# Feed-forward stage: the last group's maxima by one strided reduction, the last products by groups over four banks, the next stage's first rows and weights in the last turn

## The reference

```python
def act_quant(x):
    scale = 127.0 / jnp.clip(jnp.max(jnp.abs(x), axis=-1, keepdims=True), 1e-05)
    return jnp.clip(jnp.round(x * scale), -128, 127) / scale
...
def bit_linear(x, w):
    xq = x + jax.lax.stop_gradient(act_quant(x) - x)
    wq = w + jax.lax.stop_gradient(weight_quant(w) - w)
    return jnp.einsum('bsd,hd->bsh', xq, wq)
...
h = bit_linear(x, w1)
h = depthwise_conv1d(h.transpose(0, 2, 1), conv_w, conv_b)
h = h.transpose(0, 2, 1)
h = jax.nn.silu(h)
return bit_linear(h, w2)
...
x = x + jnp.tanh(g_ffn[0]) * _L0_ffn_ref(_layernorm(x, axis=-1), L0_ffn_w1, L0_ffn_conv_w, L0_ffn_conv_b, L0_ffn_w2)
```

## Time and profile before

| | us |
|---|---|
| three runs | 2578.31, 2588.45, 2589.29 |
| their median | 2588.45 |
| the profiled execution | 2587.03 |
| its span, first to last instruction | 2585.2 |
| feed-forward stage in it, about | 989 to 1520 |
| one turn in the loop, about | 62.5 or 63.9 |

### The profile page before, as it was taken

The page is one execution under the profiler, slowest core; times in us unless marked ns, Lnnn a source line. Parts: engine busy times, 40 slices in busy tenths (PEclk is TensorE's granted clock), DMA queues, the critical chain, the costliest instruction groups (busy, mean ns, idle before and its releaser), DMA issues. The chain is left out here.

```text
span 2585.2 us, 40732 instructions
## 1 busy us (share of the span) xinstructions
PE 2362.0 (91%) x16307; PEld 1554.4 (60%) x16348; DVE 1443.2 (56%) x1747; ACT 1060.5 (41%) x1228; POOL 608.7 (24%) x208
## 2 busy tenths in 40 slices
PE   8899999999999987899999878898878999999989
PEld 6655554555555543444444346676656888888867
DVE  7665646556565545777777567878544222222235
ACT  5444445444454442555554534444423221121223
POOL 0045546455464651000000013323210000000000
PEclk9899999999999988999999989999879999999999
DMA  9410101101010103111111131212322000000046
GB/s 298 178 40 12 49 10 48 43 11 47 10 48 11 56 15 123 34 50 49 49 53 38 38 112 44 83 56 87 106 85 82 33 32 26 22 32 32 17 156 218
DMA packets 102015, 163.73 MB, mean 63 GB/s; under 512 B 16997, under 2 KB 39525, under 8 KB 99103
## 3 DMA queue, kind: packets, MB, share of 16 engines
q1 hardware_dynamic: 95918, 150.82, 17.6%
q10 hardware_dynamic: 6000, 11.54, 1.2%
HBM read 112.63 MB, written 49.71 MB: 63 GB/s over the span
## 5 line engine op out<-in xcount | busy, mean ns | idle before, releaser
L1135 DVE TENSOR_REDUCE att_mx<-att_sn 128x2 f32<-128x1024 f32 x256 | 313.6, 1225 | 168.4 <-PE att_sn L947 166.0
L1047 ACT ACTIVATE att_num<-att_st 128x2048 f32<-128x2048 f32 x128 | 240.5, 1879 | 149.8 <-PE att_st L935 93.3
L860 POOL TENSOR_TENSOR att_es<-att_es,att_num 128x2048 f32<-128x2048 f32 x64 | 294.8, 4606 | 15.0 <-ACT att_num L1047 8.8
L856 POOL TENSOR_TENSOR att_es<-att_num 128x2048 f32<-128x2048 f32 x32 | 145.8, 4557 | 375.8 <-PE att_pj L917 366.4
L2508 ACT ACTIVATE rec_ga<-rec_g,rec_bg 128x512 f32<-128x512 f32 x84 | 57.1, 687 | 307.8 <-PE rec_g L2409 307.8
L2409 PE MATMUL rec_g<-weights_a_h,row_weights_h 128*128 128x512 f32 x384 | 152.9, 398 | 13.6 <-ACT rec_ga L2508 11.1
L2409 PE MATMUL rec_g<-weights_a_l,row_weights_h 128*128 128x512 f32 x384 | 151.7, 395 | 0.0
L2409 PE MATMUL rec_g<-weights_a_h,row_weights_l 128*128 128x512 f32 x384 | 151.5, 395 | 0.0
L947 PE MATMUL att_sn<-att_kh,att_qh 32*128 32x512 f32 x512 | 127.3, 493 | 22.7 <-DVE att_mx L1135 22.7
L1708 DVE TENSOR_TENSOR ffn_hs<-ffn_h,ffn_fb 128x1024 f32<-128x1024 f32 x64 | 78.1, 1220 | 117.5 <-PE ffn_h L1454 108.9
L561 POOL TENSOR_TENSOR ffn_ln_rstd<-ffn_ln_var,ffn_ln_power 128x4 f32<-128x4 f32 x8 | 22.0, 2755 | 484.0 <-DVE ffn_ln_var L582 484.0
(11 more groups left out here) (399 smaller groups left out, 5699.3 us busy)
## 6 DMA issues: line engine op xcount, KB each, us to landing
rows<-in_x SPq DMA_DIRECT2D x16, 1024.0 KB, 5.5
rows<-x SPq DMA_DIRECT2D x16, 1024.0 KB, 5.2
rows_b<-in_fside_BxSxS SPq DMA_DIRECT2D x8, 1024.0 KB, 7.9
heads<-att_o SPq DMA_DIRECT2D x32, 256.0 KB, 2.3
weights_b_l<-heads SPq DMA_DIRECT2D x8, 1024.0 KB, 5.2
x<-ffn_xr SPq DMA_DIRECT2D x32, 256.0 KB, 2.1
xat_xr<-x SPq DMA_DIRECT2D x8, 1024.0 KB, 5.1
out_x<-x SPq DMA_DIRECT2D x8, 1024.0 KB, 8.8
```

What stands on the lines that cost most here:

```text
L856: pool.tensor_tensor(ES[:], E[0][:], E[1][:], ALU.add).then_inc(s_sum, 1)
L860: pool.tensor_tensor(ES[:], ES[:], E[k][:], ALU.add).then_inc(s_sum, 1)
L1047: act.activation(E[k][:], st_ps[:], ACT.Exp, scale=SCALE).then_inc(s_exp, 1)
L1135: dve.tensor_reduce(MX[c % 2][:, m // 2, 2 * DH * (m % 2):2 * DH * (m % 2) + DH + 1:DH], sn_ps[:], AX, ALU.max, negate=True).then_inc(s_ma ...
```

## The change

- `absolute(b, 3)`, the ACT pass over the last group, is gone, and so is `magnitude(b, 3)` on DVE. In their place DVE folds AM first (groups 0 to 2) and then runs `last_maxima`: one `tensor_reduce` with absolute values over the last group, read as 512 rows of 4 values that lie 2048 bytes apart, into AB[:, 0], and one `tensor_tensor` of 512 elements into AM[:, 0].
- Batch 7's second product runs by groups: for each group, four matmuls into each of four banks (a, b and the two of h), behind one wait for each group.
- The next stage's `ln.moments` and `ln.scale` move from the tail into turn 7 on DVE; ACT's two high parts move ahead of `second_row(7)`; the two low parts on DVE move ahead of and behind the four `rounded`; SP issues the two weight loads ahead of the stores of batch 6.
- ACT's copy of XM into XR for batch 7 moves from ahead of the four `whole` to between the second and the third.

```diff
-        MAX_N = GROUPS + 1
+        MAX_N = GROUPS + 2
...
-            turn(B - 1, True, False, False)
             sp.wait_ge(s_h, B * PAIRS)
             for i, next_w in enumerate((next_wq, next_wo)):
                 sp.dma_start(raw[i], kxn(next_w)).then_inc(s_nextw[i], 16)
+            turn(B - 1, True, False, False)
...
+            def last_products():
+                banks = (a_ps[:], b_ps[:], h_ps[:, 0, :], h_ps[:, 1, :])
+                pe.wait_ge(s_qb, B)
+                for group in range(GROUPS):
+                    pe.wait_ge(s_quant, (B - 1) * GROUPS + group + 1)
+                    for t in range(T):
+                        for i in range(HG * group, HG * group + HG):
+                            last = pe.matmul(banks[t], SQ[:, i, t * P:t * P + P], W2[:, i, :],
+                                             start=(i == 0), stop=(i == HT - 1))
+                        if group == GROUPS - 1:
+                            last.then_inc(s_y, 1)
...
-                absolute(b, 3)
...
             turn(B - 1, True, False, False)
-            second_row(B - 1)
-            act.wait_ge(s_store, (B - 1) * T * 16)
-            act.wait_ge(s_xm, B)
-            act.activation(XR[:], XM[:], ACT.Copy).then_inc(s_xr, 1)
-            for group in range(GROUPS):
-                whole(B - 1, group)
             act.wait_ge(s_x1, B * T)
             for i, weights in enumerate((WO, O)):
                 act.wait_ge(s_nextw[i], 16)
                 act.activation(weights[0][:], raw[i], ACT.Copy).then_inc(s_nexthi, 1)
+            second_row(B - 1)
+            for group in range(GROUPS):
+                whole(B - 1, group)
+                if group == 1:
+                    act.wait_ge(s_store, (B - 1) * T * 16)
+                    act.wait_ge(s_xm, B)
+                    act.activation(XR[:], XM[:], ACT.Copy).then_inc(s_xr, 1)
...
+            def last_maxima(b):
+                dve.wait_ge(s_silu, b * HT + HT)
+                dve.tensor_reduce(AB[:, 0, :], SS[:, HT - HG:HT, :].rearrange("p m s -> p s m"), AX, ALU.max,
+                                  apply_absolute_value=True).then_inc(s_max, 1)
+                dve.wait_ge(s_max, b * MAX_N + MAX_N - 1)
+                dve.tensor_tensor(AM[:, 0, :], AM[:, 0, :], AB[:, 0, :], ALU.max).then_inc(s_max, 1)
...
                 magnitude(b, 1)
+                if not front:
+                    dve.wait_ge(s_nextx, 16)
+                    ln.moments(dve, next_rows)
...
                 scaled(b, 7)
+                if not front:
+                    ln.scale(dve, B, next_rows)
...
-                magnitude(b, 3)
                 fold(b)
+                last_maxima(b)
```

More of the change, by code:

```diff
@@ L1559, in _ @@
             second_factors(B - 1, False)
-            for t in range(T):
-                second(B - 1, t, False)
+            last_products()
         @block.scalar
@@ L1711, in magnitude @@
             def magnitude(b, group):
-                dve.wait_ge(s_abs, b * GROUPS + group + 1)
+                dve.wait_ge(s_abs, b * (GROUPS - 1) + group + 1)
                 if group > 1:
@@ L1814, in _ @@
             token_maxima(B - 1)
-            after = Steps(s_next, 0, ln.DVE_N)
-            dve.wait_ge(s_nextx, 16)
-            ln.moments(dve, after)
+            next_low(0)
             for group in range(GROUPS):
                 rounded(B - 1, group)
-            ln.scale(dve, B, after)
-            for i, weights in enumerate((WO, O)):
-                out_rows(B - 1, i, False)
-                dve.wait_ge(s_nexthi, i + 1)
-                dve.tensor_tensor(weights[1][:], raw[i], f32(weights[0][:]), ALU.subtract).then_inc(s_nextlo, 1)
-            for t in range(2, T):
+            next_low(1)
+            for t in range(T):
                 out_rows(B - 1, t, False)
```

18 lines of the change are left out of this document (13 added, 5 removed).

## The result

The changed kernel takes 2614.62 us, the median of four runs (2610.95 to 2616.48); the kernel before took 2587.15 beside it (2578.31 to 2589.29, four runs). The ratio is 1.0111, with a 95% interval of 1.0085 to 1.0137: slower by 1.1%, some 27 us. The profiled execution took 2610.95 us, with a span of 2609.1 where before's was 2585.2, so the two traces differ by 23.9 us.

The account below looks back on a forecast made before the run. The prediction took PE as the bound (busy 2362.0 of 2585.2 us), waiting in each turn for DVE's chain. 14.6 + 5.6 + 3.0 + 1.4 + 2.0 - 2.1 + 0.3 = 24.8 us on 2587.03 gave 2612, range 2591 to 2619.

Parts of the forecast that it names:

- the forecast's own mechanism: A slower strided reduction lengthens DVE's maxima chain, PE waits for it and runs at low clock behind; chance 0.50.
- Rival 1: In the maxima chain, the strided reduction runs at the contiguous rate, near 2.28 us: 2597 us in all, chance 0.32.
- Rivals 2 and 4: Contiguous-rate reduction with PE at full clock, about 2587, 0.05; tail bound by weights' parts or first rows, some 2573, 0.03.
- R, the reduction: Time of DVE's strided reduction of 2048 elements in the maxima chain: 3.76 us taken, 2.28 from below, 4.4 from above.
- the 91 ns of the small strided reduction: Excess of the trace's 128-element strided reduction over a contiguous one, taken to grow with length, giving 3.76 us.
- The chain and PE's stop: DVE's maxima chain 6.60 us, 2.09 longer; PE stands 3.5 us ahead of the transposes; 14.6 us over seven turns.
- The clock term: Convolutions behind the transposes: four more turns fall to the lower clock, 1.40 us each, 5.6 us.
- Turn 7: Last loop turn: moments cost 3.0 us of wait and 1.4 of clock, and the later fold 2.0.
- The fold's term: End of turn 7: the third `out_rows` gates the fold, so the fourth `out_rows` comes 2.0 us later.
- The tail: PE's last products run without stops, 15.9 us in place of 18.0: a gain of 2.1, with 0.3 given back.
- with unbroken work I take 4.2 us: In the last products, the full clock returns 4.2 us after PE's restart, ten matmuls at the lower clock.
- The 0.3 for the stores: In the tail, the four stores end closer together, which costs 0.3 us.

Follow-up runs that it names:

- `contiguous`: The changed kernel with the reduction over four neighbours in memory a result, not four values 2048 bytes apart: 2596.96 us, ratio to before 1.0047.
- The probes: The changed kernel with extra DVE reductions, maxima and scalings at the end of the stage, reading at various steps, in two runs; only the single operations' times are given.
- `moments_back`: The changed kernel with the next stage's moments and scalings back in the tail, the strided reduction kept: 2604.67 us, ratio to before 1.0088.
- `only_products`: The kernel before with only the last products by groups over four banks: 2587.57 us, ratio to before 1.0018.
- `gap`: The changed kernel with moments and scalings back in the tail and the maxima chain ahead of the next pass's first conversion: 2571.06 us, ratio to before 0.9949.
- `undo_maxima`: The changed kernel with the maxima of before (ACT pass and `magnitude`), the new last turn and tail kept: 2587.28 us, ratio to before 1.0022.
- `products_low`: The kernel before with last products by groups, weights' low and high parts, loads and XR copy moved; old maxima, moments in the tail: 2583.91 us, ratio 0.9993.
- `order_abs`: `products_low` with the old maxima chain moved ahead of the next pass's first conversion: 2601.25 us, ratio to before 1.0066.
- `gap_last`: `gap` with the fold and strided reduction ahead of the third output rows in the last turn: 2571.23 us, ratio to before 0.9945.

## Why the prediction was right, and where it was not

The forecast of 2612 stands 2.6 us under the median and 1 us over the profiled execution, with the forecast's own mechanism and not that of a rival. The two medians differ by 27.5 us, where 24.8 was forecast. Rival 1, the reduction at the contiguous rate, was given 2597; `contiguous` is that case and took 2596.96. Rivals 2 and 4 have nothing for them.

- **R, the reduction.** 3.64 us, forecast 3.76. Scaling the 91 ns of the small strided reduction by its length was right in kind and 3% high. The probes show why: it reads one value in each 16 bytes, from four places by turns. The Trainium skill's rule in "SBUF — State Buffer", section Door 1 (two hits in a 16-byte line are wanted, and each access to a new line pays), agrees with 2.29 us at 8 bytes and 3.74 at 16. The trace differs where the page lets 4 fp32 be stepped over for free (a step of 12 bytes already took 2.85, one of 16 bytes 3.74), and in that pairs read by turns from two far places cost nothing, though each value lies in another line than the one before (2.31). The sentence of the Trainium skill's "VectorE: DVE Perf Modes", section Mode 1×, on odd strides at a result a cycle did not hold for two operations that take 2.29 us for 2048 values in order: the reduction took 3.74 at a step of 16 bytes, the maximum of two operands 3.79. The scaling's 2.00 us does not speak against it, being below that 2.29.
- **The chain and PE's stop.** 6.48 us, forecast 6.60; PE's stop 3.35 to 3.45 us in turns 2 to 6, forecast 3.5. That nothing absorbs it was right: the chain's 1.97 us more in turn 3 are 1.97 us more of PE's stop (1.40 to 3.37). The prediction read the seven waits of the earlier trace rows as those of turns 1 to 7; they are those of turns 2 to 7 and of the tail. The sum does not suffer, since turn 1 has its own stop, which grew by 1.92. Seven stops grew by 14.1 us, forecast 14.6.
- **The clock term.** Forecast 5.6 (four turns pass from 3.40 to 4.80). All seven are slow, as said, but at lengths from 4.37 to 5.62, not 4.80: 6.7 us together. The forecast had one length for a slow convolution; why they differ was not found.
- **Turn 7.** The moments were forecast at 3.0 of wait and 1.4 of clock; `moments_back` shows 3.0 and 1.7. The fold's term was forecast at +2.0: PE's wait ahead of the last transposes grew by 1.77 (2.75 to 4.52). With the 1.55 us of a slow convolution, counted in the clock term, that is 8.0, and the stretch is 7.9 longer.
- **The tail.** This term was too large. The forecast was -2.1 with 0.3 given back, measured -1.0. The step that failed is "with unbroken work I take 4.2 us" for the return of the clock; it took 5.2 us in after and 3.2 in `moments_back`, so the products gained 1.44 and not 2.1. And the start of the products did not keep its distance to the maxima: 9.73 us behind the last transposes and not 9.29, since these ran in 1.09 us and not 0.63, behind the stop of 4.52. The 0.3 for the stores was nothing: 4.70 us from the last product to the next stage, against 4.69. `only_products` shows a term that the prediction passed over, the place of the low parts. In the change it is dealt with, but a prediction for the products alone would have been wrong by 3.9 us.
- **The sum.** 24.8 forecast, 23.9 in the traces. The stage itself lost 26.0, and 2.1 came back in code that is the same in both. Term by term, measured against forecast: stops 14.1 and 14.6, clock behind them 6.7 and 5.6, moments 4.7 and 4.4, the last chain 1.8 and 2.0, tail -1.0 and -1.8; together 26.3 against 24.8. Each is within some 1 us, and the nearness of the sum beyond that is luck. So is that of rival 1 to `contiguous`, whose trace has more of the clock's loss than the rival counted and a gain that isn't in the turns.
- **What the prediction did not ask.** It took the chain's place in DVE's order as given and priced only its length. The row with 4.64 us of idle time directly ahead was in the trace. Its own sentence, "only the length of the DVE chain counts", is right for the order as written and wrong as a finding on the kernel: `gap` has the longer chain and is the fastest.

## What to carry to other kernels

Removing a step that was hidden gains nothing by itself; what it may give is that the steps behind it can start earlier, and then the order has to be changed to use that. When an edit frees a chain from a late input, look for idle time ahead of the chain on the same engine and move the chain into it: here the same reduction, with all else alike, came out 0.9% slower than before (21 us) behind 4.6 us of idle time (`moments_back`) and 0.5% faster (13 us) inside it (`gap`). Where results are regrouped so that they come together at the end, move away what had been hidden between them.

## What the hardware showed that was not expected

- DVE's reduction reads fp32 as fast with two values in each 16 bytes as in order, and takes 60% longer with one (2.29 and 3.74 us for 2048 values; a scaling 1.23 and 2.00). Two places read by turns are free (2.31), four are not (3.62), for reductions and for two operands.
- The longer PE's stop ahead of the transposes (or, in `gap`, ahead of the convolution), the more of the convolutions behind were slow: none of turns 2 to 7 with the one stop of 1.07 us (`gap`), three of seven at 1.4 us (in before, `undo_maxima`, `only_products` and `products_low` alike), six of seven at 2.0 (`contiguous`), all seven at 3.4 (after and `moments_back`); turn 1's stop was 0.9 us longer in each of these. How much of one ran at the low level of 1.2 GHz was scattered: 4.36 to 5.62 us for the same 96 matmuls, where the full clock takes 3.40. The stop's length alone does not decide it. In `order_abs` stops of 3.1 to 3.3 us stood ahead of the products of L1454 and not of the transposes: behind them these eight matmuls took 1.90 us in turns 4, 5 and 6, at the full clock, and 2.87 to 3.59 in turns 2, 3 and 7. And behind the same stop of 2.90 us in turn 7 the second convolution took 3.40 us in `undo_maxima` and `order_abs`, 4.64 in `gap`, 4.97 in before and 6.00 in `gap_last`.
- The same code behind the stage took 1058.3 to 1065.9 us from kernel to kernel, with nothing changed in it but when it began.
